# Eight-head cross-attention: softmax denominators from two exact one-pass parts over the full array

## The chip, the cores and the metric

One NeuronCore of a Trainium2 chip runs the whole program. The time is the device time of one execution in microseconds; the number for the kernel before is the median of three runs.

## The reference, cut to what matters

The model has four layers of cross-attention, a mixer and a feed-forward part on x of 16 x 64 x 256 with a context of 16 x 1024 x 192. The change touches the cross-attention of the third and the fourth layer (L2 and L3), which compute the same with other weights:

```python
def _L2_xattn_ref(x, context, Wq, Wk, Wv, Wo, bo):
    HEADS, DIM_HEAD = 8, 64
    scale = d ** (-0.5)
    q = (x @ Wq).reshape(B, Sq, h, d).transpose(0, 2, 1, 3)
    k = (context @ Wk).reshape(B, -1, h, d).transpose(0, 2, 1, 3)
    v = (context @ Wv).reshape(B, -1, h, d).transpose(0, 2, 1, 3)
    scores = jnp.einsum('bhid,bhjd->bhij', q, k) * scale
    attn = jax.nn.softmax(scores, axis=-1)
    out = jnp.einsum('bhij,bhjd->bhid', attn, v)
    out = out.transpose(0, 2, 1, 3).reshape(B, Sq, h * d)
    return out @ Wo + bo
...
x = x + _L2_xattn_ref(_layernorm(x, axis=-1), ctx_768, ...)
```

The softmax divides by a sum over 1024 keys. The kernel divides late: it mixes the context with the exponentials, projects, and multiplies by the inverse of the sum. The change is in how that sum is made.

## The kernel before, in words

`attend_eight` is called twice, for L2 and for L3, each time as one stage with a program for every engine. Its work is cut into 32 pairs: 16 batches, two groups of four heads each. A pair has 256 query rows (4 heads x 64 positions), lying along the free dimension, and 1024 keys in 8 tiles of 128 partitions. 64 pairs run in all.

A full-precision 32-bit product leaves two records in the trace, each with a weight load of its own (PEld); L2556 has 512 products in two calls and 1024 records. A product of the type float32r is called one-pass here.

TensorE's queue for iteration p, in order:

- `scores(p)`: 8 products with 128-column weights (L2556), then 8 with half the rows (L2562).
- `project_out` (L2637), where p leaves 2 when divided by 4, from p = 6.
- `mix_wide(p - 1)`: 8 products (L2595), with the two transposes of `turn_most(p)` (L2571) at the sixth and those of `spread_top(p)` (L2577) at the eighth.
- `mix_rest(p - 1)`: 16 products with 64-column weights, in two halves of the array (L2602).
- `add_up(p - 1)`: two products of the ones, 128 partitions x 64 columns, with the 256 columns of `partial`, one for each half of the array (L2616). It waits for GpSimd's `partial_ready`. After the last pair it stands ahead of `mix_rest`.
- `project_values` (L2627 with 64-column weights, L2630 with 128), where p leaves 1 when divided by 4, from p = 5; 7 times in a call it stands behind an `add_up` and ahead of the next `scores`, once at the end.

Because `add_up(p - 1)` stands in iteration p, what follows it is mostly L2556 of iteration p + 1.

VectorE finds the largest score (L2708, twice, then L2711 and L2713), subtracts it (L2721), and inverts the sums after every second pair (L2728). ScalarE copies (L2672), takes the exponentials (L2677) and copies the mixed context (L2684, L2686). GpSimd adds the 8 tiles of exponentials into one: two additions of 128x512 (L2531), one of 128x512 (L2534) and one of 128x256 (L2538) into `partial`, of which there are two in turn. Ahead of it, once in a call, it fills the ones (L2524) and adds the bias to the tokens (L2525). From pair 8, after every fourth pair, and after pair 30, it normalises a tile of tokens for the next stage (L197, L198, L201) behind L2538.

All loads of the stage are issued by SP; none stands in what the change touches.

L1005, L993 and L980 are in another stage, the last one. They are the program's one-pass products: there the operand is split into `upper` and `lower` and both are multiplied by the same second operand; L1005 is 8 tiles of tokens x 8 chunks x 2 parts, 128 products. L594 is a helper for products; one of its forms has 8 moving columns.

Of the kernel before, what the change touches and what calls it, by code (L numbers as in the profile page):

```python
# [4 lines left out]
F32 = mybir.dt.float32  # L5
F32R = mybir.dt.float32r
U8 = mybir.dt.uint8
I32 = mybir.dt.int32
ALU = mybir.AluOpType
# [3 lines left out]
P = 128  # L13
B, S, D = 16, 64, 256
# [118 lines left out]
class Statistics:  # L133
# [9 lines left out]
    def tile(self, dve, j):  # L143
        n = self.n
        if self.ahead and j == NT - 1:
            return
        dve.bn_stats(self.raw[:, j, :], self.src[:, j, :]).then_inc(self.measured, 1)
        dve.wait_ge(self.measured, 2 * j + 1)
        dve.bn_aggr(n.mv[:, j, :], self.raw[:, j, :]).then_inc(self.measured, 1)
# [2315 lines left out]
def attend_eight(chip, X, xn, xnT, q0, q1, Wv0, Wv1, Wo, bias, first, w, ident, ahead):  # L2465
# [6 lines left out]
    HEADS = 8  # L2472
    PAIRS = B * 2
    ROWS = 2 * P
    TURN_AT, SPREAD_AT = 5, 7
    with Stage(chip) as st:
# [1 line left out]
        ct0, ct1, ctx = [first[0], st.sbuf(P, SK)], [first[1], st.sbuf(P, HALF)], [first[2], st.sbuf(P, KT, CC)]  # L2478
        probsT = [st.sbuf(P, KT, ROWS) for _ in range(2)]
        most_of, most, top, most_all = [st.sbuf(P, ROWS) for _ in range(2)], st.sbuf(P, ROWS), st.sbuf(P, 2), st.sbuf(P, ROWS)  # L2480
        quarters, halves_of, partial = st.sbuf(P, 4, ROWS), st.sbuf(P, 2, ROWS), [st.sbuf(P, ROWS) for _ in range(2)]
        ones, inverse = st.sbuf(P, S), st.sbuf(P, HEADS // 2, P)
        m0, m1 = [st.sbuf(P, HEADS, P) for _ in range(2)], [st.sbuf(P, HEADS // 2, P) for _ in range(2)]
        values = st.sbuf(P, HEADS // 2, P)
        acc_s = st.psum(P, KT, ROWS)
# [2 lines left out]
        acc_v, acc_sum = st.psum(P, HEADS // 2, P), st.psum(P, HEADS // 2, P)  # L2488
# [1 line left out]
        spare = acc_v.rearrange("p i t -> p (i t)")  # L2490
        keys_in, ctx_in = st.sems(2), st.sems(2)
        (scored, part_most, most_ready, most_turned, top_ready, top_spread, spread_copied, shifted, exp_done, adding,
         partial_ready, summed, inverse_ready, mixed, mixed_copied, values_filled, values_ready, y_filled, added,
         biased, ones_ready) = st.sems(21)
        statistics = Statistics(chip, st, X, ahead=True)
        next_norm = Ahead(chip, st, statistics, xn, NT - 1)
        first_features = acc_s[:, 0:KT // 2, :].rearrange("p (c n) r -> p c (n r)", c=DC)
# [7 lines left out]
        @block.sync  # L2505
        def _(sync):
            st.clear_other_set(sync)
            chip.load_far(sync, ahead)
            for b in range(1, B):
                x = b % 2  # L2510
                if b >= 2:
                    sync.wait_ge(scored, 4 * b - 4)
                sync.dma_start(ct0[x][:, :], w["ctxT"][b, 0:P]).then_inc(keys_in[x], 16)
                for h in range(2):
                    sync.dma_start(ct1[x][h * C1:h * C1 + C1, :], w["ctxT"][b, P:CC, halves(h)]
                                   ).then_inc(keys_in[x], 16)
                if b >= 2:
                    sync.wait_ge(mixed, 2 * b - 2)
                sync.dma_start(ctx[x][:, :, :], w["ctx"][b]).then_inc(ctx_in[x], 16)
            chip.wait_far(sync)  # L2520

        @block.gpsimd
        def _(pool):
            pool.memset(ones[:, :], 1.0).then_inc(ones_ready, 1)  # L2524
            pool.tensor_tensor(X[:, :, :], X[:, :, :], bias[:, :].unsqueeze(1).broadcast_to([P, NT, D]), ALU.add  # L2525
                               ).then_inc(biased, 1)
            for p in range(PAIRS):
                t = probsT[p % 2]
                for n in range(2):
                    pool.wait_ge(exp_done, 2 * p + n + 1)  # L2530
                    pool.tensor_tensor(quarters[:, 2 * n:2 * n + 2, :], t[:, 4 * n:4 * n + 2, :], t[:, 4 * n + 2:4 * n + 4, :],  # L2531
                                       ALU.add).then_inc(adding, 1)
                pool.wait_ge(adding, 3 * p + 2)
                pool.tensor_tensor(halves_of[:, :, :], quarters[:, 0:2, :], quarters[:, 2:4, :], ALU.add).then_inc(adding, 1)  # L2534
                pool.wait_ge(adding, 3 * p + 3)
                if p >= 2:
                    pool.wait_ge(summed, p - 1)
                pool.tensor_tensor(partial[p % 2][:, :], halves_of[:, 0, :], halves_of[:, 1, :], ALU.add  # L2538
                                   ).then_inc(partial_ready, 1)
                if p >= 8 and p % 4 == 0:  # L2540
                    next_norm.normalise(pool, range(p // 4 - 2, p // 4 - 1))
                if p == PAIRS - 2:
                    next_norm.normalise(pool, range(NT - 2, NT - 1))

        @block.tensor
        def _(pe):
# [58 lines left out]

            def add_up(p):
                g, e, at = p // 4, p % 2, p // 2 % 2 * S
                pe.wait_ge(partial_ready, p + 1)
                if p == 0:
                    pe.wait_ge(ones_ready, 1)  # L2610
                if g and p % 4 == 0:
                    pe.wait_ge(inverse_ready, 2 * g)
                if p % 4 == 2:
                    pe.wait_ge(inverse_ready, 2 * g + 1)
                for s in range(2):
                    ins = pe.matmul(acc_sum[s * S:s * S + S, 2 * e:2 * e + 2, at:at + S], ones[:, :],  # L2616
                                    partial[p % 2][:, tile(s)], start=True, stop=True)
                ins.then_inc(summed, 1)


# [1472 lines left out]
```

## Time and profile before

| | us |
|---|---|
| median of three runs | 2678.98 |
| lowest, highest | 2677.59, 2683.32 |
| the profiled execution, its own time | 2683.01 |
| its span, first to last instruction | 2681.2 |
| TensorE products busy in the span | 2526.3 |
| first call of `attend_eight`, about | 1227.5 to 1639.3 |
| second call, about | 1865.0 to 2281.8 |

The profiled execution is one of its own; its time is 2683.01 us, of which 1.8 lie outside the span. Line numbers are those of the kernel before. PE is TensorE's products, PEld its weight loads, which overlap products; DVE is VectorE, ACT ScalarE, POOL GpSimd. A bracket at the end of a row of the timeline gives the idle time of the engine just before and what ended it; "issue" is time in which it waited for nothing that the profile shows.

### The profile page before, as it was taken

How to read it: one execution, taken by the hardware profiler on the slowest of the kernel's cores; microseconds unless marked ns; L12 is line 12 of the kernel's file. 1: busy time of each engine (PE TensorE's matmuls, PEld its weight loads, DVE VectorE, ACT ScalarE, POOL GpSimd, SP SyncE). 2: the span in 40 equal slices, each digit the busy share in tenths (PEclk: the TensorE clock that was granted, in tenths of full speed). 3: DMA queues.
4: the chain of work that ended last, by engine and by line, in shares of the span. 5: the costliest groups of instructions: out<-in, count | busy, mean ns of one | idle time of the engine just before them, and what ended most of it. 6: DMA issues, size and time to landing. Idle time of an engine off the chain costs nothing. (4 is left out here: it accounts for less than half of the span.)

```text
span 2681.2 us, 47271 instructions
## 1 busy us (share of the span) xinstructions
PE 2526.3 (94%) x18434; PEld 1947.5 (73%) x18434; DVE 1451.5 (54%) x2409; ACT 1000.8 (37%) x2168; POOL 674.4 (25%) x708
## 2 busy tenths in 40 slices
PE   8889996999999899999999998997999999989999
PEld 4676993666666656876888887894888888467678
DVE  4574224777777743025555556425555454589982
ACT  2252224666666431333222221223222222477731
POOL 2102002000100011012343441202433433057833
PEclk9999998999999999999999999998999999999999
DMA  9343873111110102962112112464121220012210
GB/s 306 124 141 131 297 268 97 35 47 33 33 48 17 52 1 98 320 220 87 60 60 72 58 50 101 152 224 122 60 70 54 67 63 21 26 69 89 80 44 17
DMA packets 98668, 262.15 MB, mean 98 GB/s; under 512 B 19124, under 2 KB 45592, under 8 KB 90920
## 3 DMA queue, kind: packets, MB, share of 16 engines
q1 hardware_dynamic: 86808, 241.22, 27.2%
q0 software_dynamic: 3840, 10.49, 1.3%
q10 hardware_dynamic: 7824, 7.70, 0.9%
q8 instruction: 138, 2.26, 0.4%
q14 instruction: 58, 0.48, 0.1%
HBM read 237.18 MB, written 22.19 MB: 97 GB/s over the span
## 5 line engine op out<-in xcount | busy, mean ns | idle before, releaser
L2531 POOL TENSOR_TENSOR buf<-buf 128x512 f32<-128x512 f32 x128 | 160.1, 1270 | 473.7 <-ACT buf L2677 473.5
L2708 DVE TENSOR_REDUCE buf<-acc 128x256 f32<-128x1024 f32 x128 | 150.8, 1220 | 215.0 <-PE acc L2562 215.0
L2595 PE MATMUL acc<-buf 128*128 128x256 f32 x1024 | 257.0, 384 | 0.0
L2556 PE MATMUL acc<-buf 128*128 128x256 f32 x1024 | 236.6, 384 | 3.1 <-PEq L94 2.3
L2672 ACT COPY buf<-acc 128x256 f32<-128x256 f32 x64 | 23.8, 372 | 532.9 <-PE acc L2577 532.9
L2556 PEld LDWEIGHTS acc<-buf 128*128 128x128 f32 x1024 | 189.4, 190 | 36.5 <-issue 11.7
L2595 PEld LDWEIGHTS acc<-buf 128*128 128x128 f32 x1024 | 180.8, 190 | 33.4 <-issue 15.9
L3080 ACT ACTIVATE buf<-acc,buf 128x512 f32<-128x512 f32 x256 | 172.6, 686 | 75.2 <-DVE buf L3114 75.1
L3114 DVE TENSOR_REDUCE buf<-acc 128x1 f32<-128x512 f32 x256 | 159.0, 684 | 65.1 <-PE acc L2992 65.1
L2721 DVE TENSOR_TENSOR buf<-acc,buf 128x1024 f32<-128x1024 f32 x128 | 150.8, 1220 | 67.8 <-ACT buf L2672 67.8
L3004 PEld LDWEIGHTS acc<-identity,buf 128*128 128x128 f32 x1024 | 115.0, 141 | 84.0 <-issue 78.1
L2677 ACT ACTIVATE buf<-buf 128x1024 f32<-128x1024 f32 x128 | 135.5, 1058 | 84.5 <-DVE buf L2721 80.0
L1634 PE MATMUL acc<-buf 128*128 128x128 f32 x1312 | 157.6, 280 | 5.2 <-DMA buf<-in_L_ffn_W 3.2
L1634 PEld LDWEIGHTS acc<-buf 128*128 128x128 f32 x1312 | 155.4, 195 | 9.0 <-issue 5.1
L3128 DVE COPY buf<-acc 128x512 f32<-128x512 f32 x192 | 126.4, 685 | 56.9 <-PE acc L3004 56.6
L3511 DVE TENSOR_TENSOR_SCAN buf<-buf,acc 128x1024 f32<-128x1024 f32 x64 | 144.2, 2273 | 5.4 <-PE acc L3451 4.0
L3004 PE MATMUL acc<-identity,buf 128*128 128x128 f32 x1024 | 137.9, 277 | 6.0 <-DVE buf L3128 6.0
L2562 PE MATMUL acc<-buf 64*128 64x256 f32 x1024 | 127.9, 389 | 0.0
L2602 PE MATMUL acc<-buf 128*64 128x128 f32 x2048 | 125.8, 276 | 0.0
L2602 PEld LDWEIGHTS acc<-buf 128*64 128x64 f32 x2048 | 110.6, 137 | 20.5 <-issue 20.5
L2562 PEld LDWEIGHTS acc<-buf 64*128 64x128 f32 x1024 | 93.6, 186 | 29.7 <-issue 21.2
L3550 POOL TENSOR_TENSOR buf<-buf 128x1024 f32<-128x1024 f32 x32 | 76.9, 2424 | 99.1 <-DVE buf L3511 99.0
(464 smaller groups left out, 4807.6 us busy)
## 6 DMA issues: line engine op xcount, KB each, us to landing
buf<-in_L_ffn_W SPq DMA_DIRECT2D x52, 1024.0 KB, 6.8
buf<-in_ctx SPq DMA_DIRECT2D x48, 768.0 KB, 4.4
buf<-in_ctxT SPq DMA_DIRECT2D x64, 512.0 KB, 3.8
buf<-in_L_ffn_w SPq DMA_DIRECT2D x36, 704.0 KB
buf<-state_rows SPq DMA_DIRECT2D x32, 512.0 KB
buf<-in_ctxT SPq DMA_DIRECT2D x96, 128.0 KB, 4.0
buf<-in_L_ffn_w SPq DMA_DIRECT2D x18, 640.0 KB
buf<-in_ctxT SPq DMA_DIRECT2D x32, 256.0 KB, 5.0
```

Of the source, the lines that this page charges most:

```text
L1634: ins = pe.matmul(up(x, u, m), Wup[x][u][:, k, tile(m)], taken[x][:, k, :], start=(k == 0), stop=(k == DC - 1))
L2531: pool.tensor_tensor(quarters[:, 2 * n:2 * n + 2, :], t[:, 4 * n:4 * n + 2, :], t[:, 4 * n + 2:4 * n + 4, :], ALU.add).then_inc(adding, 1)
L2556: pe.matmul(acc_s[:, n, :], ct0[x][:, tile(key_tile(n))], q0[:, b, 4 * y:4 * y + 4, :], start=(n % 2 == 0), stop=False)
L2562: ins = pe.matmul(acc_s[:, 4 * n + 2 * h + i, :], ct1[x][at, tile(k)], q1[at, b, 4 * y:4 * y + 4, :], start=False, stop=(i == 1))
L2595: pe.matmul(acc_m[:, 0:ROWS], ctx[x][:, key_tile(n), 0:P], probsT[y][:, n, :], start=(n == 0), stop=(n == KT - 1))
L2602: ins = pe.matmul(acc_m[s * C1:s * C1 + C1, 2 * P:3 * P], ctx[x][:, key_tile(n), P:CC], probsT[y][:, n, tile(s)], start=(n == 0), stop=(n ...
L2708: dve.tensor_reduce(most_of[n][:, :], acc_s[:, 4 * n:4 * n + 4, :].rearrange("p k r -> p r k"), AX.X, ALU.max).then_inc(part_most, 1)
L2721: dve.tensor_tensor(probsT[p % 2][:, 4 * n:4 * n + 4, :], acc_s[:, 4 * n:4 * n + 4, :], most_all[:, :].unsqueeze(1).broadcast_to([P, 4, RO ...
L3004: ins = pe.transpose(acc_t[i % 2][:, k, :], probs[s % 2][:, i, tile(k)], ident[:, :])
L3080: act.activation(probs[s % 2][:, i, :], acc_s[i][:, :], ACT.Exp, bias=negmax[:, x, h, i:i + 1], accum_out=total[:, x, h, i:i + 1]).then_in ...
L3114: dve.tensor_reduce(negmax[:, s // 2 % 2, s % 2, i:i + 1], acc_s[i][:, :], AX.X, ALU.max, negate=True).then_inc(max_ready, 1)
L3511: dve.tensor_tensor_scan(state[n % STATES][:, :], decay[n % 2][:, :, :].rearrange("p b s -> p (b s)"), acc_d[n % 2][:, :], 0.0, ALU.mult, ...
```

## The change

GpSimd's sum of a pair (`partial`, now one buffer) is split by two further instructions: a copy rounds it to float32r (`upper`), and a subtraction leaves the rest (`lower`), each in two buffers in turn. Both are exact together. `add_up` multiplies both by the ones in one-pass products. The ones are now two matrices of 128 x 128: one with ones in the first 64 columns and zeros in the others, one the other way round, so that a product fills all 128 partitions of the sum and the two halves are accumulated: four products for a pair in place of two. `add_up` waits for `parts_ready` in place of `partial_ready`. The ones are filled by four instructions on zeros in place of one memset.

```diff
--- before.py
+++ after.py
@@ -2478,8 +2478,9 @@
         ct0, ct1, ctx = [first[0], st.sbuf(P, SK)], [first[1], st.sbuf(P, HALF)], [first[2], st.sbuf(P, KT, CC)]
         probsT = [st.sbuf(P, KT, ROWS) for _ in range(2)]
         most_of, most, top, most_all = [st.sbuf(P, ROWS) for _ in range(2)], st.sbuf(P, ROWS), st.sbuf(P, 2), st.sbuf(P, ROWS)
-        quarters, halves_of, partial = st.sbuf(P, 4, ROWS), st.sbuf(P, 2, ROWS), [st.sbuf(P, ROWS) for _ in range(2)]
-        ones, inverse = st.sbuf(P, S), st.sbuf(P, HEADS // 2, P)
+        quarters, halves_of, partial = st.sbuf(P, 4, ROWS), st.sbuf(P, 2, ROWS), st.sbuf(P, ROWS)
+        upper, lower = ([st.sbuf(P, ROWS, dtype=F32R) for _ in range(2)] for _ in range(2))
+        ones, inverse = st.sbuf(P, 2, P, dtype=F32R), st.sbuf(P, HEADS // 2, P)
         m0, m1 = [st.sbuf(P, HEADS, P) for _ in range(2)], [st.sbuf(P, HEADS // 2, P) for _ in range(2)]
         values = st.sbuf(P, HEADS // 2, P)
         acc_s = st.psum(P, KT, ROWS)
@@ -2490,8 +2491,8 @@
         spare = acc_v.rearrange("p i t -> p (i t)")
         keys_in, ctx_in = st.sems(2), st.sems(2)
         (scored, part_most, most_ready, most_turned, top_ready, top_spread, spread_copied, shifted, exp_done, adding,
-         partial_ready, summed, inverse_ready, mixed, mixed_copied, values_filled, values_ready, y_filled, added,
-         biased, ones_ready) = st.sems(21)
+         partial_ready, upper_ready, parts_ready, summed, inverse_ready, mixed, mixed_copied, values_filled, values_ready, y_filled, added,
+         biased, ones_ready) = st.sems(23)
         statistics = Statistics(chip, st, X, ahead=True)
         next_norm = Ahead(chip, st, statistics, xn, NT - 1)
         first_features = acc_s[:, 0:KT // 2, :].rearrange("p (c n) r -> p c (n r)", c=DC)
@@ -2521,7 +2522,10 @@
 
         @block.gpsimd
         def _(pool):
-            pool.memset(ones[:, :], 1.0).then_inc(ones_ready, 1)
+            for s in range(2):
+                for x in range(2):
+                    ins = pool.tensor_scalar(ones[:, s, x * S:x * S + S], chip.zeros[:, 0:S], float(x == s), None, ALU.add)
+            ins.then_inc(ones_ready, 1)
             pool.tensor_tensor(X[:, :, :], X[:, :, :], bias[:, :].unsqueeze(1).broadcast_to([P, NT, D]), ALU.add
                                ).then_inc(biased, 1)
             for p in range(PAIRS):
@@ -2535,8 +2539,13 @@
                 pool.wait_ge(adding, 3 * p + 3)
                 if p >= 2:
                     pool.wait_ge(summed, p - 1)
-                pool.tensor_tensor(partial[p % 2][:, :], halves_of[:, 0, :], halves_of[:, 1, :], ALU.add
+                pool.tensor_tensor(partial[:, :], halves_of[:, 0, :], halves_of[:, 1, :], ALU.add
                                    ).then_inc(partial_ready, 1)
+                pool.wait_ge(partial_ready, p + 1)
+                pool.tensor_copy(upper[p % 2][:, :], partial[:, :]).then_inc(upper_ready, 1)
+                pool.wait_ge(upper_ready, p + 1)
+                pool.tensor_tensor(lower[p % 2][:, :], partial[:, :], upper[p % 2][:, :].bitcast(F32), ALU.subtract
+                                   ).then_inc(parts_ready, 1)
                 if p >= 8 and p % 4 == 0:
                     next_norm.normalise(pool, range(p // 4 - 2, p // 4 - 1))
                 if p == PAIRS - 2:
@@ -2605,16 +2614,17 @@
 
             def add_up(p):
                 g, e, at = p // 4, p % 2, p // 2 % 2 * S
-                pe.wait_ge(partial_ready, p + 1)
+                pe.wait_ge(parts_ready, p + 1)
                 if p == 0:
                     pe.wait_ge(ones_ready, 1)
                 if g and p % 4 == 0:
                     pe.wait_ge(inverse_ready, 2 * g)
                 if p % 4 == 2:
                     pe.wait_ge(inverse_ready, 2 * g + 1)
-                for s in range(2):
-                    ins = pe.matmul(acc_sum[s * S:s * S + S, 2 * e:2 * e + 2, at:at + S], ones[:, :],
-                                    partial[p % 2][:, tile(s)], start=True, stop=True)
+                for n, part in enumerate((upper[p % 2], lower[p % 2])):
+                    for s in range(2):
+                        ins = pe.matmul(acc_sum[:, 2 * e:2 * e + 2, at:at + S], ones[:, s, :],
+                                        part[:, tile(s)], start=(n == 0 and s == 0), stop=(n == 1 and s == 1))
                 ins.then_inc(summed, 1)
```

## Rows read from the trace of the kernel before

**Rows 1.** The page's list of engines: busy us, share of the span, instructions.
```profile
PE 2526.3 (94%) x18434; PEld 1947.5 (73%) x18434; DVE 1451.5 (54%) x2409; ACT 1000.8 (37%) x2168; POOL 674.4 (25%) x708
```

**Rows 2.** Busy time of each engine in windows of the first call.
```profile
1250.00:1628.00 378.00, 378.00 (x2868) 312.69 (x2864) 202.88 (x224) 87.47 (x151) 148.99 (x141) 1.00 0.18 57
1250.09:1261.88 11.79, 11.79 (x90) 9.66 (x88) 5.57 (x7) 2.92 (x6) 4.49 (x4) 1.00 0.01 1
```

**Rows 3.** Waits of the weight loads, 1240 to 1628 us: total, times, longest.
```profile
PEld acc L2602 <- issue: 10.3, 31, 0.3
...
PEld acc L2556 <- issue: 3.9, 23, 0.2
...
PEld acc L2630 <- issue: 1.2, 7, 0.2
```

**Rows 4.** Timeline of steady pairs: start us, us, engine, line.
```profile
1239.44 2.50 POOL L2531 TENSOR_TENSOR buf<-buf 128x512 f32<-128x512 f32 x2 [7.31 <-ACT buf L2677]
...
1247.35 0.30 PEld L2595 LDWEIGHTS acc<-buf 128*128 128x128 f32 x2
...
1247.98 1.73 PEld L2602 LDWEIGHTS acc<-buf 128*64 128x64 f32 x32 [0.33 <-issue]
...
1249.67 0.25 PEld L2616 LDWEIGHTS acc<-buf 128*64 128x64 f32 x4
...
1250.09 3.32 PEld L2556 LDWEIGHTS acc<-buf 128*128 128x128 f32 x16 [0.17 <-issue]
...
1254.37 0.73 POOL L2538 TENSOR_TENSOR buf<-buf 128x256 f32<-128x256 f32 x1
1254.93 2.36 DVE L2708 TENSOR_REDUCE buf<-acc 128x256 f32<-128x1024 f32 x2 [4.51 <-PE acc L2562]
1255.67 2.02 PEld L2595 LDWEIGHTS acc<-buf 128*128 128x128 f32 x10 [0.33 <-issue]
...
1257.32 0.43 DVE L2711 TENSOR_TENSOR buf<-buf 128x256 f32<-128x256 f32 x1
1257.80 0.28 PEld L2571 LDWEIGHTS acc<-identity,buf 128*128 128x128 f32 x2
...
1261.46 0.25 PEld L2616 LDWEIGHTS acc<-buf 128*64 128x64 f32 x4
```

**Rows 5.** Timeline around sums that the value projection follows.
```profile
1600.66 0.25 PEld L2616 LDWEIGHTS acc<-buf 128*64 128x64 f32 x4
...
1600.88 0.91 PEld L2627 LDWEIGHTS acc<-buf 128*64 128x64 f32 x16
```

**Rows 6.** Groups of weight loads over the whole span.
```profile
L2556 PEld LDWEIGHTS acc<-buf 128*128 128x128 f32 x1024 | 189.4, 190 | 36.5 <-issue 11.7 <-DVE buf L2721 1.7
...
L2616 PEld LDWEIGHTS acc<-buf 128*64 128x64 f32 x256 | 16.1, 137 | 2.1 <-POOL buf L2538 2.1
L1005 PEld LDWEIGHTS acc<-buf 128*128 128x128 f32 x128 | 15.5, 192 | 0.1
```

**Rows 7.** Timeline, weight loads of L594 and L1005 in a row.
```profile
1046.02 0.97 PEld L594 LDWEIGHTS acc<-first_weights,xn_features 128*128 128x128 f32 x8 [0.16 <-DVE xn_features L512]
...
2662.60 5.57 PEld L1005 LDWEIGHTS acc<-buf 128*128 128x128 f32 x45
```

**Rows 8.** GpSimd's groups, shapes kept apart.
```profile
L1052 POOL TENSOR_TENSOR buf<-xn_features,buf 128x512 fp32r<-128x512 f32 x24 | 33.3, 1392 | 64.0 <-DVE buf L1017 64.0
...
L201 POOL TENSOR_SCALAR xn_tokens<-x_tokens,buf 128x256 f32<-128x256 f32 x20 | 24.6, 1235 | 1.7
...
L2937 POOL TENSOR_TENSOR buf<-buf 128x8 f32<-128x8 f32 x32 | 6.5, 203 | 23.2 <-ACT buf L3087 23.2
```

**Rows 9.** Timeline of the last pair of the first call.
```profile
1632.58 0.73 POOL L2538 TENSOR_TENSOR buf<-buf 128x256 f32<-128x256 f32 x1
1633.36 0.20 PEld L2616 LDWEIGHTS acc<-buf 128*64 128x64 f32 x4 [1.06 <-POOL buf L2538]
...
1633.52 1.78 PEld L2602 LDWEIGHTS acc<-buf 128*64 128x64 f32 x32
```

## The prediction

> **What bounds the kernel now.** I read the page first: TensorE's products are busy 94% of the span and its weight loads 73% [rows 1]. The change touches one helper, used in two stretches, so I asked for windows there. In the first call, from 1250 to 1628 us, TensorE's products are busy 378.00 of 378.00 us at a granted clock of 1.00 (the 2.4 GHz level), and one steady pair takes 11.79 us, all of it busy [rows 2]. VectorE has 5.57 us of work in such a pair and GpSimd 4.49. So between the first and the last pair of a call TensorE is the clock of the stage; what its queue gains or loses comes out at the end, and another engine matters only where it makes TensorE wait.
>
> "Busy" here hides drains of the array. The waits of the weight loads show them: 31 gaps of 0.33 us ahead of L2602, and gaps of 0.17 us ahead of L2556, 23 times, and of L2630, 7 times [rows 3, 4]. They stand only where the shape of the tile in the array changes: from 128-column weights to 64-column ones at L2602, and back at L2556 or L2630. Between two lines with 64-column weights (L2602 to L2616, L2616 to L2627) there is none [rows 4, 5]. This, and not the columns that are multiplied, is what I price the change by.
>
> **Cost of the products today.** Records with 64-column weights come in twos, one for each half of the array: 32 loads of L2602 take 1.73 us, so (1.73 - 0.14)/15 = 0.106 us for two [rows 4]. The sums at L2616 are 256 records [rows 6]: two products in two records each, for 64 pairs. So a pair pays two steps of 0.106 = 0.212 us. The last such step begins at 1249.67 + 0.11 = 1249.78, and the full-array L2556 at 1250.09: a switch back costs 0.31 us from load to load, with or without the sums [rows 4].
>
> **The one-pass products.** The change issues four products with 128-column weights and 128 moving columns. What sets their pace is not shown for this shape; two rows bound it. L1005 is one-pass, with the same weights and 256 moving columns: (5.57 - 0.19)/44 = 0.122 us a load [rows 6, 7]. L594 with 128-column weights and only 8 moving columns still takes (0.97 - 0.19)/7 = 0.111 us a load [rows 7], so there the load is the pace. A load of L1005 lasts 192 ns, a full-precision load of 128 columns 190 and one of 64 columns 137 [rows 6]: what counts there is the columns, and the one-pass kind is no shorter. I take 0.115, between 0.111 and 0.122. Four are 0.46 us against 0.212: the one pass saves moving columns, but four wide loads replace two steps of paired narrow ones.
>
> A rule of the Trainium skill speaks for the change here: "TensorE: Matmul & The Clock Gate", section Weight-path perf modes, says a faster weight load is on when there are 128 weights and the type is not FP32; the ones are of a type that isn't named FP32. The 192 ns of L1005 [rows 6] speak against it. By that rule the time is that of the second rival below.
>
> **Where the drains go.** Of the 64 pairs' sums the last of each call and the one before it are told of below; behind 46 of the other 60 the queue goes on with full-array L2556. There the switch only moves from behind the sums to ahead of them: cost 0.46 - 0.212 = 0.248 us, times 46 = 11.4 us. Behind the other 14 (7 in each call) the queue goes on with L2627, which has 64-column weights [rows 5]. Before, the sums fitted in with no switch. Now there is one in (0.31 - 0.106 = 0.204) and one out. A switch out is 0.52 us behind a 256-column full-precision record: L2595's last load begins 0.11 us after 1247.35 and L2602's first at 1247.98 [rows 4]. That includes 0.21 us of streaming (10 records from 1255.67 to 1257.80), of which a one-pass record of 128 columns needs a quarter, 0.05. So 0.36, less the 0.115 of an ordinary step: 0.245. Sum 0.248 + 0.204 + 0.245 = 0.70 us, times 14 = 9.8 us. Bounds for the switch out: 0.21 to 0.52.
>
> **GpSimd.** Two instructions more per pair, each behind a wait on the one before it. The subtraction is like L2538, 0.73 us, and with an output of the one-pass type L1052 takes 1.39 against about 1.25 for L2531 at the same 512 elements [rows 4, 8], so 0.80. The copy of 256 elements with one input has no row: below by the 0.20 of L2937 on 8 elements, above by the 1.24 of L201, which does two operations with scalars on the same 256 [rows 8]. I take 0.6, nearer a plain pass than L201's. Two handshakes of 0.07 each, a little over the 0.05 from L2538's end at 1633.31 to TensorE's load [rows 9]. Together 1.54 us, 1.1 to 2.2.
>
> In a steady pair this is covered: L2538 ends at 1255.10 and the sums are loaded at 1261.46 [rows 4], so 6.3 us of cover; without it a pair would pay 1.5. The wait for the old sums that stands ahead of L2538, and the tokens' normalisation queued behind the subtraction, have the same slack. The four fills of the ones replace one, before GpSimd's own first wait of 7.31 us at 1239.44 [rows 4]; four at L201's 1.24 would be 5.0 us. Nothing for them.
>
> In the last pair of a call it is not covered. There the sums stand ahead of L2602, and TensorE already waits 1.06 us for L2538 [rows 9]. The 1.54 us go on top. GpSimd's start there hangs on work that stands ahead of the sums of the pair before, so what those lose is taken up by this wait: that is why 46 and 14 count 60 pairs. The four loads and the switch out then cost 3 x 0.115 + 0.36 = 0.70 where 0.16 us stood (1633.36 to 1633.52). Tail: 1.54 + 0.54 = 2.1 us, twice: 4.2. Behind it come L2602, ScalarE's copies, L2627 and the end of the stage, in a chain, so it is not given back.
>
> Another rule of the skill, "GPSIMD Engine Reference", section Specifications, says that GpSimd shares its memory interfaces with VectorE and contends with VectorE's instructions that read two inputs from there. L2711 is such an instruction; the timing below decides.
>
> **Sum.** 11.4 + 9.8 + 4.2 = 25.4 us. The profiled execution took 2683.0 us beside a span of 2681.2, and would become 2708.4. It lies 4.0 us above the median of 2679.0, so for the median I forecast 2704.4, +0.95%.
>
> **Rivals.**
> First, VectorE is slowed by GpSimd's added 1.5 us. L2711 ends at 1257.75 and the transpose L2571 that needs it loads at 1257.80 [rows 4]: 0.05 us of slack in each pair, so this decides from 0.05 us. GpSimd's new work would run until 1256.6, beside L2708 but before L2711's 1257.32. Ten per cent more on L2708's 2.36 us would be 0.24, less 0.05, times 60: +11 us, 2716. Against it: the two L2708 took 2.36 us although L2538 ran beside their first 0.17 us. By the skill's rule only L2711 would suffer, and it is clear by 0.7 us.
>
> Second, the wide one-pass load is quick, and the moving columns set the pace: L1005's 0.122 less the 0.053 of 128 columns, 0.067 to 0.07. Then 46 x 0.056 + 14 x 0.55 + 2 x 1.94 = 14 us, 2693. A switch into one-pass products at no cost would give nearly the same, 46 x 0.044 + 14 x 0.49 + 4.2 = 13 us. Against the quick load: the 192 ns of rows 6. Against the free switch: the gaps of rows 3.
>
> Third, the other sign: the one-pass loads are prepared under the running products, so neither switch costs anything and four steps take 0.212 us as before. Then the 46 switches are saved, 46 x 0.204 = 9.4, the 14 cost nothing, the tail 1.6 twice: 9.4 - 3.2 = 6 us faster, 2673. It breaks even where a step takes about 0.077 us. For it: no row shows a step between column tiles and one-pass products. Against it: every other change of tile shape here has its gap, 31 of 31.
>
> Fourth, the change doesn't do what it says, and a product of this type still takes two records. Then four more steps a pair, 0.46 x 62 = 28 us on top, 2733. Against it: L1005 has 128 records for 128 products in the code (8 tiles, 8 chunks, two parts).
>
> **How the numbers follow.** Forecast 0.73; quick load or free switch in, 0.10; slowed VectorE 0.09; nothing drains 0.05; two records 0.03. The forecast's own range takes the pace from 0.111 to 0.122 (-0.7 to +1.3), the switch out from 0.21 to 0.52 (14 times, -2.1 to +2.2) and GpSimd's 1.1 to 2.2 twice (-0.9 to +1.3): 2700 to 2710. The range reaches down over the second rival, 2691, and above to 2712; the two upper rivals and the third lie outside. The measurement tells about 0.2%, 5.4 us, from no change: slower holds the forecast and rivals one, two and four, 0.95; the third's 0.05 is split into faster, 0.03, and, near its break-even, the same, 0.02.
>
> **What would show it.** In the changed profile: L2616 (moved by some lines) with 256 records of 128x128 weights, its steps at 0.11 to 0.12 us; a gap of about 0.17 us ahead of it and none ahead of L2556; a gap ahead of L2627; a steady pair of 12.04 us in place of 11.79; TensorE still busy for all of it; one wait on GpSimd of some 2.3 us in each call. VectorE's L2708 still at 1.22 us each. I am wrong if the steps take 0.07, if no gap precedes the sums, or if TensorE waits at L2571.

## The result and the profile after

The changed kernel took 2706.06 us, median of four runs (2703.01 to 2717.82), against 2681.15 us for the kernel before beside it: a ratio of 1.0101, 95% interval 1.0080 to 1.0123. The forecast was 2704.4 us. The profiled execution is the longest of the four, 2717.82 us with a span of 2716.0; its mean granted clock was 0.974 of the 2.4 GHz level, that of the other three 0.979 to 0.984. Its first call starts at 1237.56 us where the kernel before had 1227.50, in stages that the change doesn't touch, and up to there the granted clock averages 0.96 against 0.98; in the kernels below that start lies anywhere from 1220.6 to 1230.4. One execution each of two kernels below (7810.39 us of the one with wide full-precision products, 6526.19 us of the one whose parts are not used) lies far outside and is left out of their ratios; what held them up the record doesn't show. I therefore read the two stages by themselves. **Stage time** is from the first load of the scores to the first load of the closing idle products (L380):

| kernel | first call, us | second call, us |
|---|---|---|
| before | 413.34 | 413.34 |
| changed | 425.73 | 424.46 |

That is 12.4 and 11.1 us, 23.5 in all. The changed kernel's windows, to set beside [rows 2]: between the first and the last pair TensorE's products are again busy for all of 378.00 us, and the steady pair has gone from 11.79 to 12.02 us.

```profile
1250.00:1628.00 378.00, 378.00 (x2796) 311.44 (x2795) 198.07 (x214) 85.05 (x146) 180.19 (x198) 1.00 0.18 59
1260.38:1272.40 12.02, 12.02 (x90) 9.89 (x90) 5.57 (x7) 2.92 (x6) 5.61 (x6) 1.00 0.01 1
```

Its timeline in a steady pair, beside [rows 4]: the sums (now L2626) follow L2611, the narrow mixing products, with a gap of 0.17 us; the scores (L2565) follow with no gap. The four loads take 0.44 us to the next load.

```profile
1258.04 1.73 PEld L2611 LDWEIGHTS acc<-buf 128*64 128x64 f32 x32 [0.33 <-issue]
...
1259.94 0.52 PEld L2626 LDWEIGHTS acc<-buf 128*128 128x128 f32 x4 [0.17 <-issue]
...
1260.38 3.33 PEld L2565 LDWEIGHTS acc<-buf 128*128 128x128 f32 x16
```

Where the value projection follows (L2637, beside [rows 5]) the sums have a gap ahead, and the narrow weights behind them begin 0.59 us after their first load:

```profile
1306.10 1.73 PEld L2611 LDWEIGHTS acc<-buf 128*64 128x64 f32 x32 [0.33 <-issue]
...
1308.00 0.52 PEld L2626 LDWEIGHTS acc<-buf 128*128 128x128 f32 x4 [0.17 <-issue]
...
1308.59 0.85 PEld L2637 LDWEIGHTS acc<-buf 128*64 128x64 f32 x16
```

From one pair's first scores to the next such a pair takes 13.55 us in the kernel before and 14.07 in the changed one, 0.53 more when the times are not rounded. Five of the seven in each call take another 0.09 (14.17), for a reason that the experiments come to.

```profile
1285.45 3.32 PEld L2556 LDWEIGHTS acc<-buf 128*128 128x128 f32 x16 [0.17 <-issue]
...
1299.00 3.33 PEld L2556 LDWEIGHTS acc<-buf 128*128 128x128 f32 x16
```

```profile
1296.43 3.33 PEld L2565 LDWEIGHTS acc<-buf 128*128 128x128 f32 x16
...
1310.50 3.33 PEld L2565 LDWEIGHTS acc<-buf 128*128 128x128 f32 x16
```

The waits of its weight loads in the first call, beside [rows 3]: a gap stands ahead of L2626, none ahead of the scores (L2565), which had 23. The first transposes of a pair, L2580, now wait for VectorE's L2721 (L2711 in the kernel before). One of these six waits, of 0.96 us at the start of the call, the kernel before has as well; the other five, of 0.26 to 0.28 us, are new, and a sixth stands near the end of the call.

```profile
PEld acc L2626 <- issue: 5.0, 29, 0.2
PEld acc L2580 <- DVE buf L2721: 2.3, 6, 1.0
```

The last pair of the first call, and then of the second, beside [rows 9]: the wait for GpSimd is 2.08 us in place of 1.06.

```profile
1653.39 0.72 POOL L2547 TENSOR_TENSOR buf<-buf 128x256 fp32r<-128x256 f32 x1
1654.17 0.52 PEld L2626 LDWEIGHTS acc<-buf 128*128 128x128 f32 x4 [2.08 <-POOL buf L2547]
...
1654.76 2.45 PEld L2611 LDWEIGHTS acc<-buf 128*64 128x64 f32 x32
...
2304.13 0.52 PEld L2626 LDWEIGHTS acc<-buf 128*128 128x128 f32 x4 [2.08 <-POOL buf L2547]
...
2304.72 1.73 PEld L2611 LDWEIGHTS acc<-buf 128*64 128x64 f32 x32
```

The group of the sums' loads, beside [rows 6], and the changed kernel's two new groups on GpSimd, the subtraction and the copy, beside [rows 8]:

```profile
L2626 PEld LDWEIGHTS acc<-buf 128*128 128x128 f32 x256 | 33.4, 190 | 14.8 <-issue 10.6 <-POOL buf L2547 4.2
```

```profile
L2547 POOL TENSOR_TENSOR buf<-buf 128x256 fp32r<-128x256 f32 x64 | 46.3, 724 | 5.1
...
L2545 POOL CAST buf<-buf 128x256 fp32r<-128x256 f32 x64 | 25.3, 396 | 4.2
```

That the two parts together are exact, as the title and the change have it, none of the runs here measures; the times don't rest on it.

### The profile page after: what moved, and what is told of

Read it like the earlier page. It is cut to its first block and busy times, and to the rows that moved or that the text cites. A ratio compares the mean times of both kernels' runs of the same rounds, so it can differ in the third digit from the quotient of the medians.

```text
span 2716.0 us, 47405 instructions
## 1 busy us (share of the span) xinstructions
PE 2566.6 (94%) x18434; PEld 1977.3 (73%) x18434; DVE 1455.8 (54%) x2409; ACT 1000.2 (37%) x2168; POOL 748.8 (28%) x842
## 5 line engine op out<-in xcount | busy, mean ns | idle before, releaser
L2718 DVE TENSOR_REDUCE buf<-acc 128x256 f32<-128x1024 f32 x128 | 150.8, 1220 | 217.8 <-PE acc L2571 217.8
L2604 PE MATMUL acc<-buf 128*128 128x256 f32 x1024 | 257.0, 384 | 0.0
L2565 PE MATMUL acc<-buf 128*128 128x256 f32 x1024 | 234.2, 382 | 3.1 <-PEq L94 2.3
L2565 PEld LDWEIGHTS acc<-buf 128*128 128x128 f32 x1024 | 189.6, 190 | 28.6 <-issue 3.9
L2604 PEld LDWEIGHTS acc<-buf 128*128 128x128 f32 x1024 | 180.8, 190 | 33.4 <-issue 15.9
L2571 PE MATMUL acc<-buf 64*128 64x256 f32 x1024 | 127.9, 389 | 0.0
L2611 PE MATMUL acc<-buf 128*64 128x128 f32 x2048 | 126.8, 277 | 0.0
L2611 PEld LDWEIGHTS acc<-buf 128*64 128x64 f32 x2048 | 111.2, 137 | 20.7 <-issue 20.5
L2571 PEld LDWEIGHTS acc<-buf 64*128 64x128 f32 x1024 | 93.6, 186 | 29.7 <-issue 21.2
```

Source lines behind the costliest of these rows:

```text
L2565: pe.matmul(acc_s[:, n, :], ct0[x][:, tile(key_tile(n))], q0[:, b, 4 * y:4 * y + 4, :], start=(n % 2 == 0), stop=False)
L2571: ins = pe.matmul(acc_s[:, 4 * n + 2 * h + i, :], ct1[x][at, tile(k)], q1[at, b, 4 * y:4 * y + 4, :], start=False, stop=(i == 1))
L2604: pe.matmul(acc_m[:, 0:ROWS], ctx[x][:, key_tile(n), 0:P], probsT[y][:, n, :], start=(n == 0), stop=(n == KT - 1))
L2611: ins = pe.matmul(acc_m[s * C1:s * C1 + C1, 2 * P:3 * P], ctx[x][:, key_tile(n), P:CC], probsT[y][:, n, tile(s)], start=(n == 0), stop=(n ...
L2718: dve.tensor_reduce(most_of[n][:, :], acc_s[:, 4 * n:4 * n + 4, :].rearrange("p k r -> p r k"), AX.X, ALU.max).then_inc(part_most, 1)
```

## The experiments

Each was compared with the kernel before on the same chip. Ratios that lie this near to each other are read together with the stage times, which agree within 0.03 us between the two calls in every kernel but two (the last section). A kernel with one run has no interval, and its stage times come from that run's trace.

| kernel | ratio to before, 95% interval | stage, first and second call, us |
|---|---|---|
| wide full-precision products | 1.0062, 1.0036 to 1.0087 | 423.04, 423.04 |
| parts made, not used | 1.0011, 1.0001 to 1.0021 | 414.60, 414.61 |
| sums ahead of the narrow mixing | 1.0070, 1.0049 to 1.0090 | 421.25, 421.23 |
| normalisation ahead of the split | one run, 2699.34 us | 424.07, 424.04 |
| upper part only | 1.0016, 1.0001 to 1.0031 | 416.17, 416.18 |
| before, last sums behind | 0.9987, 0.9974 to 0.9999 | 412.39, 412.39 |
| one-pass products in halves | one run, 2730.69 us | 438.79, 437.52 |
| narrow one-pass, one half | one run, 2688.17 us | 417.42, 417.42 |

### Is it the width or the type?

The kernel before with the wide ones alone (the `ones` are declared and filled as in the changed kernel):

```diff
...
-                    ins = pe.matmul(acc_sum[s * S:s * S + S, 2 * e:2 * e + 2, at:at + S], ones[:, :],
-                                    partial[p % 2][:, tile(s)], start=True, stop=True)
+                    ins = pe.matmul(acc_sum[:, 2 * e:2 * e + 2, at:at + S], ones[:, s, :],
+                                    partial[p % 2][:, tile(s)], start=(s == 0), stop=(s == 1))
```

> The kernel before with the wide ones alone: two full-precision products with 128-column weights over all partitions, four records a pair, no split by GpSimd. Stage time is from the first load of the scores to the load of the closing idle products: 413.3 us before, 424.5 in the changed kernel's second call. Theory (the width of the weights and the switches of tile shape cost, not the type): a steady pair of 12.02 us, a gap of 0.17 us ahead of the sums and none behind, stage +9.8 us without GpSimd's part, ratio to before about 1.0073. Rival (the one-pass type costs): a pair within 0.05 us of 11.79 and a ratio within 0.2% of 1.

The stage grew by 9.7 us. In its timeline the sums (L2619) and the scores (L2559) look as in the changed kernel, and a pair is 12.01 to 12.02 us:

```profile
1248.44 0.52 PEld L2619 LDWEIGHTS acc<-buf 128*128 128x128 f32 x4 [0.17 <-issue]
...
1248.89 3.33 PEld L2559 LDWEIGHTS acc<-buf 128*128 128x128 f32 x16
...
1260.90 3.33 PEld L2559 LDWEIGHTS acc<-buf 128*128 128x128 f32 x16
```

In such a pair two full-precision products in four records and four one-pass products cost TensorE the same. Where the value projection follows, the full-precision ones cost 0.05 us more: 0.58 over the kernel before in each of the seven pairs, against 0.53. So with wide ones the type brings next to nothing and costs nothing; the width and the switches cost.

### GpSimd's part alone

The kernel before with the copy and the subtraction made and waited for, and the sums still narrow and from the unsplit `partial`:

```diff
...
+                pool.wait_ge(partial_ready, p + 1)
+                pool.tensor_copy(upper[p % 2][:, :], partial[p % 2][:, :]).then_inc(upper_ready, 1)
+                pool.wait_ge(upper_ready, p + 1)
+                pool.tensor_tensor(lower[p % 2][:, :], partial[p % 2][:, :], upper[p % 2][:, :].bitcast(F32), ALU.subtract
+                                   ).then_inc(parts_ready, 1)
...
-                pe.wait_ge(partial_ready, p + 1)
+                pe.wait_ge(parts_ready, p + 1)
```

> The kernel before with GpSimd's copy and subtraction added and waited for, but TensorE still takes the unsplit sum in narrow full-precision products. Theory (GpSimd costs only at the last pair and where the tokens' normalisation now runs beside VectorE's joining of the maxima): a steady pair of 11.79 us; the wait at the last pair goes from 1.06 to 2.3 us; five or six waits of 0.2 to 0.3 us a call at the first transposes; stage +2.2 us, ratio about 1.0016. Rival (GpSimd's work slows VectorE in every pair and makes TensorE wait there): pairs above 11.85 us and a stage of +5 us or more, ratio 1.004 or more.

The stage grew by 1.26 us and not 2.2. All of it is the wait at the last pair, here L2622, in the list of waits; every other pair takes what it took before:

```profile
PEld acc L2622 <- POOL buf L2544: 2.3, 1, 2.3
```

The waits at the transposes that I expected are not there. In its timeline VectorE's L2717 starts 0.05 us ahead of the normalisation L201 (0.01 to 0.04 in the other pairs), and there it is mainly GpSimd that is slowed, 1.50 us for L201 in place of 1.24, where nobody waits for it; L2717 takes 0.42 to 0.46.

```profile
1343.11 0.42 DVE L2717 TENSOR_TENSOR buf<-buf 128x256 f32<-128x256 f32 x1
1343.16 1.50 POOL L201 TENSOR_SCALAR xn_tokens<-x_tokens,buf 128x256 f32<-128x256 f32 x1
1343.59 0.28 PEld L2577 LDWEIGHTS acc<-identity,buf 128*128 128x128 f32 x2
```

### Where the switches are

The changed kernel with the sums between the wide and the narrow mixing products in every pair:

```diff
-                    if p == PAIRS:
-                        add_up(p - 1)
-                        mix_rest(p - 1)
-                    else:
-                        mix_rest(p - 1)
-                        add_up(p - 1)
+                    add_up(p - 1)
+                    mix_rest(p - 1)
```

> The changed kernel with the sums of every pair between the wide and the narrow mixing products, so that no switch of tile shape is added. Theory (switches cost by what streams ahead of them): a pair of 11.86 us also where the value projection follows (0.44 for four loads, less 0.21 and less 0.15 for a switch behind a short product in place of a long one); stage about 418, +4.6 on before; ratio to before 1.0035. Rival (switches are no part of the cost, or a change to the one-pass type has its own gap wherever it stands): stage stays above 422, ratio above 1.007.

Stage 421.2, 3.2 under the changed kernel's second call but 3.2 over my number; the ratio of 1.0070 lies at the rival's bound. The timeline (wide mixing L2604, sums L2626, narrow mixing L2611):

```profile
1260.41 0.30 PEld L2604 LDWEIGHTS acc<-buf 128*128 128x128 f32 x2
...
1260.74 0.63 PEld L2626 LDWEIGHTS acc<-buf 128*128 128x128 f32 x4
...
1261.44 1.73 PEld L2611 LDWEIGHTS acc<-buf 128*64 128x64 f32 x32
```

From L2604's two loads to L2611 it is 1.03 us; in the kernel before it was 0.63 (1247.35 to 1247.98, [rows 4]). So from load to load a pair pays 0.40 for the sums here and had paid 0.21; the whole pair went from 11.79 to 11.96, 0.18 more when the times are not rounded, and not the 0.08 that I had expected. My expectation took 0.15 off for a switch behind a short product and forgot that the long record of L2604 streams all the same, only earlier: the first two loads of the sums are 0.21 us apart, the others 0.11. So this forecast missed, by a term of its own sum. What it said of the pairs with a value projection, that they no longer pay for an added switch, came out: the two of them in each call in which nothing else happens pay 0.18 like the others (0.53 in the changed kernel). The other five pay 0.31 to 0.33, because VectorE's joining of the maxima (L2717) is slowed to 0.64 to 0.66 us there, which the next experiment is about. The seven pairs together give back 2.2 of the 3.2 us, the others 1.2, and the end of the call takes 0.2 more. The ratio lies at the rival's bound, but no gap stands ahead of L2626 behind L2604, so one-pass products have no gap of their own wherever they stand.

### The slowed joining of the maxima

In the changed kernel, close to the end of the second call, the normalisation L201 starts at 2292.78 and VectorE's L2721 beside it takes 0.60 us, not 0.43; the transposes wait 0.27 us:

```profile
2292.78 1.23 POOL L201 TENSOR_SCALAR xn_tokens<-x_tokens,buf 128x256 f32<-128x256 f32 x1
2293.01 0.60 DVE L2721 TENSOR_TENSOR buf<-buf 128x256 f32<-128x256 f32 x1
2293.66 0.20 PEld L2580 LDWEIGHTS acc<-identity,buf 128*128 128x128 f32 x2 [0.27 <-DVE buf L2721]
```

The changed kernel with the normalisation ahead of the copy:

```diff
                 pool.wait_ge(partial_ready, p + 1)
+                if p >= 8 and p % 4 == 0:
+                    next_norm.normalise(pool, range(p // 4 - 2, p // 4 - 1))
                 pool.tensor_copy(upper[p % 2][:, :], partial[:, :]).then_inc(upper_ready, 1)
...
-                if p >= 8 and p % 4 == 0:
-                    next_norm.normalise(pool, range(p // 4 - 2, p // 4 - 1))
```

> The changed kernel with the normalisation of a tile of tokens ahead of GpSimd's copy and subtraction in place of behind them (but for the last tile). Theory (the slowed joining of the maxima, up to 0.61 us against 0.43, comes from the normalisation that runs beside it): it lasts 0.43 us in all but the pair before the last, the waits of 0.27 us at the first transposes are gone but for one, stage -0.8 us against 424.5. Rival (they come from TensorE's changed timing): five to six waits a call stay.

The stage lost 0.4 us, half of what I expected, and the waits stayed, shorter (0.21 us), so the expectation failed in both its parts. Now the copy and the subtraction stand beside L2721, which takes 0.53, and the subtraction itself 0.78 in place of 0.72:

```profile
1340.59 1.25 POOL L201 TENSOR_SCALAR xn_tokens<-x_tokens,buf 128x256 f32<-128x256 f32 x1
...
1341.79 0.40 POOL L2547 CAST buf<-buf 128x256 fp32r<-128x256 f32 x1
1341.93 0.53 DVE L2721 TENSOR_TENSOR buf<-buf 128x256 f32<-128x256 f32 x1
1342.27 0.78 POOL L2549 TENSOR_TENSOR buf<-buf 128x256 fp32r<-128x256 f32 x1
1342.52 0.20 PEld L2580 LDWEIGHTS acc<-identity,buf 128*128 128x128 f32 x2 [0.21 <-DVE buf L2721]
```

So other work of GpSimd's than the normalisation can slow L2721 too. But it isn't any overlap that does. In the kernel with the upper part only (below) the normalisation starts earlier and runs beside the whole of the addition, there L2718, and both keep their times:

```profile
1336.09 1.24 POOL L201 TENSOR_SCALAR xn_tokens<-x_tokens,buf 128x256 f32<-128x256 f32 x1
...
1336.77 0.43 DVE L2718 TENSOR_TENSOR buf<-buf 128x256 f32<-128x256 f32 x1
```

That holds for all 14 such meetings in that kernel and for the 14 in the kernel with halved products, where L201 starts 0.53 to 0.82 us ahead of the addition. In the changed kernel it starts 0.22 or 0.23 us ahead in 12 of 14, and the addition takes 0.59 to 0.61. What counts is when they meet; why, stays open. The rival, that TensorE's changed timing makes the waits, is answered by the wide full-precision kernel: it has the same steady pair of 12.01 to 12.02 us, its addition (L2714) takes 0.42 or 0.43 us in all 64 pairs, and no transpose waits but the first of each call, as before.

The price in the changed kernel is 0.09 us in five pairs of a call (14.17 us in place of 14.08; with the normalisation ahead, where the wait is 0.21, all seven take 14.08 to 14.10), and 0.10 us at the end of a call: 1.1 us for both calls.

The rule of the Trainium skill that the prediction weighed ("GPSIMD Engine Reference", section Specifications) puts contention on VectorE instructions that have two inputs in the shared memory. The trace agrees so far as that L2721, with two such inputs, is the one that is slowed, and L2718 of the changed kernel, the search for the largest score, which reads the products' accumulators, kept its 1.22 us beside GpSimd's copy and subtraction; the 28 meetings without a loss show that having two inputs is not enough.

### Half of the products

The changed kernel without `lower`:

```diff
...
-                pool.wait_ge(upper_ready, p + 1)
-                pool.tensor_tensor(lower[p % 2][:, :], partial[:, :], upper[p % 2][:, :].bitcast(F32), ALU.subtract
-                                   ).then_inc(parts_ready, 1)
...
-                pe.wait_ge(parts_ready, p + 1)
+                pe.wait_ge(upper_ready, p + 1)
...
-                for n, part in enumerate((upper[p % 2], lower[p % 2])):
+                for n, part in enumerate((upper[p % 2],)):
...
```

> The changed kernel without the lower part: two wide one-pass products a pair, and GpSimd's copy but not its subtraction. It leaves the sum's rounding error in. Theory (each wide load costs 0.11 us, each switch its gap): a steady pair of 11.80 us, as before (0.31 + 2 x 0.11 against 0.52); where the value projection follows +0.36; wait at the last pair 1.53 us; stage 416.7 us against 413.3 before and 424.5 changed. Rival (the one-pass products or GpSimd's work cost as such): a steady pair above 11.85 us and a stage above 418.

Stage 416.2, 0.5 under the expectation, and a steady pair as before: 2.11 us from L2608, the narrow mixing, to L2562, the scores, where it had been 1247.98 to 1250.09, 2.11 as well. The pairs with a value projection pay 0.31 us each for the added switch in and out, and nothing else.

```profile
1252.89 1.73 PEld L2608 LDWEIGHTS acc<-buf 128*64 128x64 f32 x32 [0.33 <-issue]
...
1254.79 0.30 PEld L2623 LDWEIGHTS acc<-buf 128*128 128x128 f32 x2 [0.17 <-issue]
...
1255.00 3.33 PEld L2562 LDWEIGHTS acc<-buf 128*128 128x128 f32 x16
```

### Loads or columns

The changed kernel with each one-pass product in two of 64 columns:

```diff
-                for n, part in enumerate((upper[p % 2], lower[p % 2])):
-                    for s in range(2):
-                        ins = pe.matmul(acc_sum[:, 2 * e:2 * e + 2, at:at + S], ones[:, s, :],
-                                        part[:, tile(s)], start=(n == 0 and s == 0), stop=(n == 1 and s == 1))
+                for i in range(2):
+                    for n, part in enumerate((upper[p % 2], lower[p % 2])):
+                        for s in range(2):
+                            ins = pe.matmul(acc_sum[:, 2 * e + i, at:at + S], ones[:, s, :],
+                                            part[:, s * P + i * S:s * P + i * S + S], start=(n == 0 and s == 0),
+                                            stop=(n == 1 and s == 1))
```

> The changed kernel with each of the four one-pass products cut in two of 64 moving columns: the same columns in all, twice the weight loads. Theory (the loads set the pace): eight steps of 0.11 us, a steady pair of 12.45 us, stage 438 us against 424.5. Rival (the moving columns set it): unchanged, 12.01 and 424.5.

As expected: as many columns, twice the loads (L2627), eight steps in 0.89 us, a pair of 12.46 us.

```profile
1265.27 0.97 PEld L2627 LDWEIGHTS acc<-buf 128*128 128x128 f32 x8 [0.17 <-issue]
...
1266.16 3.33 PEld L2565 LDWEIGHTS acc<-buf 128*128 128x128 f32 x16
...
1278.62 3.33 PEld L2565 LDWEIGHTS acc<-buf 128*128 128x128 f32 x16
```

### Narrow and one-pass

The changed kernel with ones of 64 columns, all sums in the lower half of the partitions (the `ones` are declared and filled to fit):

```diff
...
-                        ins = pe.matmul(acc_sum[:, 2 * e:2 * e + 2, at:at + S], ones[:, s, :],
-                                        part[:, tile(s)], start=(n == 0 and s == 0), stop=(n == 1 and s == 1))
+                        ins = pe.matmul(acc_sum[0:S, 2 * e:2 * e + 2, at:at + S], ones[:, :],
+                                        part[:, tile(s)], start=(n == 0 and s == 0), stop=(n == 1 and s == 1))
...
-                dve.reciprocal(inverse[:, :, at], acc_sum[:, :, at]).then_inc(inverse_ready, 1)
+                dve.reciprocal(inverse[0:S, :, at], acc_sum[0:S, :, at])
+                dve.reciprocal(inverse[S:P, :, at], acc_sum[0:S, :, at]).then_inc(inverse_ready, 1)
```

> The changed kernel with ones of 64 columns: four narrow one-pass products a pair, all into the lower half of the partitions, and the inverse taken twice from there. It mixes the sums of the two halves, so its output is another. Theory (the width of the loads and the switches are the whole cost): four steps of 0.053 us with no gap, a steady pair of 11.79 us, stage 414.6 us, all of it the last pair's wait of 2.3 us. Rival (one-pass products cost as such): a pair of 11.9 us or more, a stage of 417 or more.

Half right. The loads (L2623) come every (0.31 - 0.14)/3 = 0.06 us, so with half the width of the weights, and the same moving columns, the loads come about twice as fast, and a steady pair is 11.81 us. But there is a gap of 0.17 us ahead of them, although they are as narrow as the mixing products before, and none ahead of the scores (L2562):

```profile
1249.29 0.31 PEld L2623 LDWEIGHTS acc<-buf 128*64 128x64 f32 x4 [0.17 <-issue]
...
1249.52 3.32 PEld L2562 LDWEIGHTS acc<-buf 128*128 128x128 f32 x16
...
1261.33 3.32 PEld L2562 LDWEIGHTS acc<-buf 128*128 128x128 f32 x16
```

So the queue passes to these products as it does to full-array ones. The stage is 417.4, 2.8 over my number, and most of that is the seven pairs with a value projection, which pay 0.32 us each for the switch in and out. At least three readings remain: the one-pass kind always takes the whole array; a change of type out of narrow full-precision products has a gap of its own; or the gap comes from using one half of the array alone behind products that use both in turn. Against the second: between wide full-precision and one-pass products no gap appears in either direction (L2604 to L2626 above, L2626 to L2565 in the changed kernel). Against the third: no gap stands where these products give way to the full array. Neither is settled. Narrow one-pass products in both halves were not run, so whether a form of the change costs nothing on TensorE stays open.

### A version faster than both

The kernel before with the last pair's sums behind the narrow mixing products:

```diff
-                    if p == PAIRS:
-                        add_up(p - 1)
-                        mix_rest(p - 1)
-                    else:
-                        mix_rest(p - 1)
-                        add_up(p - 1)
+                    mix_rest(p - 1)
+                    add_up(p - 1)
```

> The kernel before with the sums of the last pair behind the narrow mixing products as in every other pair. Theory: the wait of 1.06 us for GpSimd is gone and nothing takes its place, since the projection of the values needs the mixed context, not the sums; stage 412.4 us against 413.3, in all 1.8 us less, 0.07%, which the trace shows and the time can't. Rival (the inverse comes too late and VectorE's last product of values waits for it): stage 413.3 or more.

Stage 412.4, 0.95 less a call, as expected. That is 1.9 us or 0.07% of the whole; the ratio of 0.9987, its interval just clear of 1, says 0.13%, so the trace and not the ratio is what shows the gain. GpSimd's L2538 now ends under the mixing products (L2602), and the inverse (L2724) is done at 1635.87, before VectorE's last product of values, L2729, which begins at 1636.77 and waits for TensorE's L2630:

```profile
1631.82 0.73 POOL L2538 TENSOR_TENSOR buf<-buf 128x256 f32<-128x256 f32 x1
1631.87 1.73 PEld L2602 LDWEIGHTS acc<-buf 128*64 128x64 f32 x32 [0.33 <-issue]
...
1634.11 1.76 DVE L2724 RECIPROCAL buf<-acc 128x256 f32<-128x256 f32 x1 [6.39 <-PE acc L2616]
...
1636.77 0.69 DVE L2729 TENSOR_TENSOR buf<-acc,buf 128x512 f32<-128x512 f32 x1 [0.91 <-PE acc L2630]
```

## Why the prediction was right

The mechanism held on TensorE, step by step; one of the things named as signs of being wrong did come true, a wait of TensorE at the transposes, and it is small. In the table the terms of the sum are for both calls. "Measured" is the growth of the pairs, from one pair's first load of the scores to the next one's, and of the rest of the call behind the last pair's scores.

| term | forecast, us | measured, us |
|---|---|---|
| 46 steady pairs | 11.4 (0.248 each) | 10.4 (0.2265 each) |
| 14 pairs with a value projection | 9.8 (0.70 each) | 7.4 (0.53 each) |
| last pairs | 4.2 (2.1 each) | 3.3 (1.64 each: 1.26 for GpSimd, 0.38 for loads and switch) |
| overlap with L2721 | none | 1.1 |
| clock in the first call's last pair | none | 1.3 |
| sum | 25.4 | 23.5 |

That the sums lie 1.9 us apart is in part luck. The terms that the forecast has come to 21.1 us, 4.3 less than it gives them, and 2.4 us come from two things that it put at nothing.

- **Pace of the loads.** Taken as 0.115, measured 0.11: the lower bound, from L594 with 8 columns, was right. Products of 8, 64 and 128 columns all step by 0.11 us, so at these sizes the load sets the pace; L1005's 0.122 goes with its 256 columns. The Trainium skill's rule of the faster weight load ("TensorE: Matmul & The Clock Gate", section Weight-path perf modes) would have 128 weights of a type other than FP32 load faster; it is not seen for float32r, whose loads at L2626 last 190 ns, as long as the full-precision ones.
- **Where the drains go.** The gap moved from ahead of the scores to ahead of the sums, 0.17 us, as stated. The switch out was taken as 0.36 and is 0.59 - 0.33 = 0.26 behind a one-pass record of 128 columns: the most mis-sized term of the 14 pairs, 0.10 of the 0.17 us by which each came out below the forecast. Another 0.05 comes back right behind it, where the 16 loads of the value projection take 0.85 us in place of 0.91 [rows 5]; the forecast had no such term.
- **GpSimd.** Copy 0.40 us, forecast 0.6; subtraction 0.72, forecast 0.80. With 0.07 and 0.08 of handshake that is 1.27 us, forecast 1.54, and the kernel with the parts made and not used grew by 1.26 a call. TensorE's wait grew by less, from 1.06 to 2.08, forecast 2.3, because the sums of the pair before take 0.23 of it up, as the prediction said. In the other pairs nobody waits for GpSimd's work, as stated.
- **What the prediction missed.** It gave the normalisation behind the subtraction "the same slack" and looked only at who waits for it. Moved by a little over 1 us, it came to lie beside L2721, which has 0.05 us of slack, and TensorE waits at L2580 (L2571 before) in six pairs of each call. The first rival had the right instruction and the wrong reason to dismiss it: it checked the new instructions against L2711, but not the ones that they push back. It held in 12 of 64 pairs and cost 1.1 us, where it had priced 11.
- **The rivals.** The second (a quick load) falls with the pace and with the halved columns, and its other form (a free switch in) with the gap ahead of L2626. The third (no drains) falls with the gap ahead of L2626. The fourth (two records) falls with its 256 records for 256 products.

The runs' medians differ by 24.9 us, the two stages of the profiled executions by 23.5, of which 1.3 is the clock in a call that no other execution of the changed kernel has a trace of. With four executions of the changed kernel up to 15 us apart, the nearness of 24.9 to the forecast's 25.4 says no more than the stages do.

## What to carry to other kernels

Two loads of 64 columns, one for each half of the array, took 0.106 us together here, as much as one load of 128 columns (0.11). Widening the weights to save passes over the moving columns gives that up: four loads at 0.11 us replaced two steps of 0.106. Count the switches of tile shape before and after an edit in the queue's order: one that only moved was free here, and one in and out that was added cost 0.31 us, more than the 0.23 that the products added. And when instructions are put ahead of others on a covered engine, look at what the pushed ones now run beside and at what moment, not only at who waits for them.

## What the runs showed of the hardware that I had not expected

**The clock behind a short stop.** In the changed kernel's first call TensorE waits 2.08 us at the last pair, and then the granted clock falls to 0.78 and 0.65 of the 2.4 GHz level in the next two windows, so part of each was at 1.2 GHz, and is back at 1.00 in the third. The windows' columns are the busy time of the five engines, clock, DMA share, GB/s.

```profile
1654.00:1657.00 3.00, 2.83 (x34) 2.76 (x36) 1.76 (x1) 0.00 (x0) 0.12 (x1) 0.78 0.00 0
1657.00:1660.00 3.00, 2.36 (x25) 1.79 (x22) 0.00 (x0) 2.33 (x5) 0.00 (x0) 0.65 0.00 0
1660.00:1663.00 3.00, 2.15 (x14) 1.83 (x13) 0.69 (x1) 0.76 (x2) 0.00 (x0) 1.00 0.00 0
```

L2611's 32 loads take 2.45 us in place of 1.73, and that call is 1.3 us longer than the second, whose wait is as long and whose clock stays at 1.00. The kernel with the halved products had the same in its first call (0.55 and 0.88 in two windows of 3 us, 438.79 against 437.52 us), behind a wait of only 1.64 us, and not behind the same wait in its second; the four other kernels with a wait of 2.1 to 2.3 us there did not have it in either call, nor did the kernels with 1.06 and 1.5. So the length of the wait alone doesn't decide it here; what does stays open.

**Who is slowed.** Where GpSimd's normalisation (L201, by itself 1.24 us) and VectorE's addition of two inputs (by itself 0.43) run side by side, the loss depends on when they meet, and falls on one or the other:

| L201 starts | addition, us | L201, us | kernel |
|---|---|---|---|
| 0.01 to 0.05 us behind | 0.42 to 0.46 | 1.48 to 1.53 | parts not used |
| 0.04 to 0.12 ahead | 0.43 to 0.46 | 1.48 to 1.50 | changed and sums ahead, once in each call |
| 0.16 to 0.18 ahead | 0.64 to 0.66 | 1.23 or 1.24 | sums ahead |
| 0.22 or 0.23 ahead | 0.59 to 0.61 | 1.23 or 1.24 | changed |
| 0.53 to 0.82 ahead | 0.42 or 0.43 | 1.23 to 1.25 | upper part only, halved products |

Between 0.12 and 0.16 us the loss changes sides, and from 0.53 us there is none. The traces show no reason for it.
